# GpSimd's order in a slot: image normalising moved ahead of the finishes, and 24 gathers dealt out as 2, 4, 4, 4, 4, 4, 2

## The reference

```python
xn  = _gn(x)                                  # every channel of every image: (x - mean) / sqrt(var + 1e-5)
y   = conv7x7(xn, dilation 5, padding 15)     # 32 channels -> 1
imp = sigmoid(gelu(batchnorm(y)))             # importance of every pixel
xs  = xn * imp
idx = sort(top_k(imp, 192))                   # per image, in order of the pixel
tok = xs[idx] + pos[idx]                      # 192 tokens of 32 channels
t1  = ln(tok + attention(tok))                # 8 heads of 4 channels
t2  = ln(t1 + ffn(t1))
xn'      = xn
xn'[idx] = t2                                 # the tokens written back over their pixels
out = x + xn'
```

## Time and profile before

| | |
|---|---|
| median of 3 runs | 1338.59 us (1338.28 to 1342.16) |
| the profiled execution's own time | 1343.39 us |
| its span | 1341.5 us |
| mean granted TensorE clock | 0.869 of full |
| PE busy | 984.7 us (73%) |
| DVE busy | 904.1 us (67%) |
| POOL busy | 680.8 us (51%) |
| ACT busy | 662.5 us (49%) |
| moved by DMA | 246.88 MB, mean 184 GB/s |

### The profile page before, as it was taken

One profiled execution on the slowest core, in us unless ns is written; L12 is line 12 of the kernel. 1 busy time (PEld: TensorE's weight loads), 2 busy tenths in 40 slices (PEclk: granted clock), 3 DMA queues, 4 the chain that ended last, 5 costly groups with the idle time before them and its releaser, 6 DMA issues. The chain is left out here.

```text
span 1341.5 us, 21567 instructions
## 1 busy us (share of the span) xinstructions
PE 984.7 (73%) x6440; PEld 761.9 (57%) x6440; DVE 904.1 (67%) x2483; ACT 662.5 (49%) x1466; POOL 680.8 (51%) x949
## 2 busy tenths in 40 slices
PE   1397776688878978887888788877675676476647
PEld 1265555377656756775677667755553554355424
DVE  8145678678768867886788768975786675344523
ACT  1254342266436655765466546653653465256423
POOL 1043222822665386638663876286528547652553
PEclk9698897799879988999899979997987799599755
DMA  9488986575556888798879877855354454536558
GB/s 202 120 262 235 250 235 162 152 180 145 143 138 182 230 229 205 214 261 235 196 206 267 226 202 196 243 167 122 103 148 123 107 154 109 130 96 178 158 177 273
DMA packets 181223, 246.88 MB, mean 184 GB/s; under 512 B 70741, under 2 KB 77141, under 8 KB 181109
## 3 DMA queue, kind: packets, MB, share of 16 engines
q1 hardware_dynamic: 170613, 238.46, 65.9%
q10 hardware_dynamic: 2304, 4.65, 1.6%
q0 software_dynamic: 8192, 2.40, 1.3%
HBM read 123.61 MB, written 121.80 MB: 183 GB/s over the span
## 5 line engine op out<-in xcount | busy, mean ns | idle before, releaser
L534 PE MATMUL cv<-X,w_conv 128*128 128x330 f32 (+1 forms) x1024 | 315.3, 434 | 41.6 <-POOL X L974 36.7
L1018 POOL TENSOR_SCALAR res<-res,mom 128x440 f32<-128x440 f32 (+1 forms) x256 | 157.3, 616 | 329.7 <-DVE res L1314 321.2
L842 ACT ACTIVATE wgt<-ib,eps_col,mom 128x440 f32<-128x440 f32 (+1 forms) x256 | 176.5, 697 | 153.2 <-PE ib L581 144.9
L871 ACT ACTIVATE pr<-sc,least 128x192 f32<-128x192 f32 x384 | 140.6, 419 | 214.2 <-DVE least L1278 213.4
L534 PEld LDWEIGHTS cv<-X,w_conv 128*128 128x128 f32 x1024 | 196.1, 208 | 80.8 <-issue 43.4
L814 ACT COPY xt<-xb 110x512 f32<-110x512 f32 x225 | 132.7, 590 | 146.2 <-PE xb L518 110.3
L518 PE MATMUL xb<-cst,X 128*110 128x128 f32 x900 | 153.7, 298 | 68.8 <-ACT xt L814 48.6
L1314 DVE SCALAR_TENSOR_TENSOR res<-tr,mom,wgt 128x440 f32<-128x440 f32 (+1 forms) x192 | 122.4, 643 | 101.2 <-PE tr L568 94.6
L653 PE MATMUL sc<-k_b,qm 128*128 128x192 f32 x768 | 169.4, 346 | 20.2 <-ACT k_b L859 7.8
L666 PE MATMUL pp<-cst,pr 128*96 128x128 f32 x768 | 123.1, 284 | 66.9 <-ACT pr L871 49.5
L518 PEld LDWEIGHTS xb<-cst,X 128*110 128x110 f32 x900 | 105.9, 143 | 96.2 <-ACT xt L814 53.1
(11 more groups left out here) (173 smaller groups left out, 1476.7 us busy)
## 6 DMA issues: line engine op xcount, KB each, us to landing
table<-xt SPq DMA_DIRECT2D x240, 224.0 KB, 3.9
rt<-table SPq DMA_DIRECT2D x240, 224.0 KB, 4.5
out<-res SPq DMA_DIRECT2D x320, 137.5 KB, 2.9
X<-in_x SPq DMA_DIRECT2D x58, 412.5 KB, 6.1
X<-in_x SPq DMA_DIRECT2D x58, 343.8 KB, 5.2
conv_rows<-cvr SPq DMA_DIRECT2D x64, 188.0 KB
y<-conv_rows SPq DMA_DIRECT2D x64, 165.4 KB
out<-res SPq DMA_DIRECT2D x64, 68.8 KB, 2.9
```

Source lines behind the costliest of these rows:

```text
L534: last = mm(cv[:, 0:CUT[half]], w_conv[:, 4 * q + z], X[:, m % XI, at0:at0 + CUT[half]], start=z == 0, stop=z == 3)
L842: last = A(wgt[:, n % 2, at0:at0 + w], ib[:, at0:at0 + w], ACT.Identity, scale=mom[:, NB * g + b, 2:3], bias=eps_col[:, 1:2])
L871: last = A(pr[:, unit % 2, 2 * m + t, :], sc[:, k % 2, K * t:K * t + K], ACT.Exp, scale=-1.0, bias=least[:, k % 2, t:t + 1])
L1018: last = gp.tensor_scalar(v, v, 1.0, mom[:, NB * g + b, 0:1], ALU.mult, ALU.add)
```

## The change

GATHERS becomes (2, 4, 4, 4, 4, 4, 2): seven slots, phases 14 to 20. In GpSimd's loop the normalise stands first in the slot, ahead of finish, masked, norm_last, gather, scatter and split. No instruction is added or taken away, and no semaphore changes.

```diff
-        GATHER, GATHERS = 74, (3, 3, 3, 3, 3, 3, 3, 3)
+        GATHER, GATHERS = 74, (2, 4, 4, 4, 4, 4, 2)
...
                 if s == 27:
                     pool.wait_ge(dve_set, upto(dve_set, 0, 2))
                     gp.tensor_tensor(bn[:, 7:8], bn[:, 7:8], eps_col[0:H, 0:1], ALU.pow).then_inc(bn_rstd, 1)
+                for part in range(3):
+                    for g, b, n in images(s, NORMAL[part]):
+                        normalise(g, b, part)
                 for g, n in at(s, BACK, U):
                     finish(g, n)
...
                 for k in range(3):
                     for g, n in at(s, SPLIT[k]):
                         split(g, k)
-                for part in range(3):
-                    for g, b, n in images(s, NORMAL[part]):
-                        normalise(g, b, part)
```

## The result

| | before | after |
|---|---|---|
| median of 10 runs, same chip | 1341.55 us | 1348.99 us |
| lowest to highest | 1338.28 to 1343.11 | 1338.65 to 1351.67 |
| ratio after/before, 95% interval | | 1.0048 [1.0026, 1.0070] |
| profiled execution, its span | 1343.39, 1341.5 | 1349.58, 1347.8 |
| mean granted TensorE clock | 0.869 | 0.875 |

The changed kernel is slower by 0.48%: about 6.4 us by the ratio, 7.4 by the two medians. The forecast was 1336.0, the range ended at 1343.6. Of the 13 us between forecast and measurement, 3 lie in the base: the forecast started from the median of three runs of the kernel before, 1338.59, and ten runs give 1341.55. The rest is the effect of the change, forecast at -2.6.

What follows compares the result with a forecast made beforehand. No engine is full; work passes between engines each slot, with TensorE and VectorE waiting on GpSimd around the gathers. Terms -1.9 - 1.2 - 0.7 + 0.3 + 0.9 = -2.6 us from 1338.6 gave 1336.0 us, range 1330.5 to 1343.6.

Steps and rivals of the forecast that it cites:

- The scatters: Phase 5: second image's first third ahead of the last two scatters holds SyncE 2.6 us, delaying the search's map; +0.9 us.
- The prediction's own sign of being wrong: TensorE's wait falling over 1 us per group, or waits for table stores, loads back or the map in several groups.
- SyncE's hold comes through in full: Wait for the scatters at phase 6: 2.6 us in each of groups 0 to 3, 10.4; 1345.5 us, 11%.
- Fourth image: Phase 20, groups 2 to 5: first third normalised 0.48 us earlier, shortening TensorE's wait; -1.9 us over four groups.
- Group 1's second third: One normalise less stands ahead of it on GpSimd, so TensorE's 1.53 us wait nearly goes; -1.2 us.
- The gains as a sum: All forecast effects with SyncE's hold absorbed, so without the +0.9 of the scatters; -3.5 us.
- Group 0's later thirds: Group 0's normalising during the gathers: same as group 1, next to no wait on the second third; counted at nothing.
- Last gather: Groups 6 and 7, where the embedding waits for tokens: one finish less ahead; -0.7 in group 7, +0.3 in group 6.
- The rule on VectorE and GpSimd: Two-input VectorE instructions and GpSimd's SBUF reads exclude each other, so moved normalises could hold VectorE; put at nothing.
- the rival that asked for it once in each of six groups: Normalise holds an awaited VectorE instruction, 1.26 us once in each of groups 0 to 5; 1343.6 us, 4%.
- Clock kept up: Rival: shorter waits, mainly group 1's, keep TensorE's clock up, 2.8 us; with SyncE's hold absorbed 1332.3 us, 18%.

Runs made afterwards that it cites:

- the third experiment: The changed kernel with the second image's three normalises put back at the end of their slots; 1334.83 us, 0.9942 of the kernel before.
- the fourth experiment: The kernel before with only the second image's normalises moved to the front of their slots; 1353.88 us, 1.0092 of the kernel before.
- the gathers alone: The kernel before with only the gathers dealt out as 2, 4, 4, 4, 4, 4, 2, normalises last; 1364.71 us, 1.0180 of the kernel before.
- the move alone: The kernel before with all normalises first in their slots, gathers left at eight slots of three; 1344.28 us, 1.0015 of the kernel before.

## Why the prediction was wrong

- **The step that failed is "The scatters"**: +0.9 us for SyncE's hold. Moving the second image's normalises is worth 14 us taken away and 12 added on the first chip. The mechanism, its place and its victim (the map, VectorE's search) were named; the size was wrong, three times over. The prediction's own sign of being wrong, waits for the map in several groups, is there: three. First, SyncE is held longer than 2.6. Power, copies and normalise took 3.10 us (550.84 to 553.94), the finish 1.08 instead of 0.63, so the last scatter moved by 3.6 against VectorE's work, in groups 2 and 3 as well; in group 1 its landing took 1.4 longer too: 5 us. Second, I held this against slack read from before's schedule (1.2 of SyncE's idle time, 0.3 at the map). But the other steps of the change bring VectorE forward, by 6.6 us until slot 156, and what it asks for must come forward with it; slack against a schedule that moves is not slack. So group 2, with 2.3 us of idle time, lost 2.13 us, not 0.3, and group 3 lost 1.40. Third, the clock: the standstill of 4.94 us was followed by 6.8 us of work at 0.50, and from slot 156 to 165 the changed kernel lost 9.1 us where the wait by itself is 4.9. How much of the rest is the clock was not tried apart.
- **The rival "SyncE's hold comes through in full"**, 1345.5 us at 11%, named the right mechanism, and at +6.9 us came near the result's 6.4. That is luck, since two errors cancel: a hold of 10.4 us where the experiments show 12 to 14, and gains of 3.5 us where they show 7.8. And from the base of 1338.6 its 1345.5 lies 3.5 us under the measured 1348.99.
- **Fourth image, -0.48 a group**: right to the tenth, 0.22 us wait included. **Group 1's second third, -1.2**: right in the wait, 1.53 and a weight load's 1.94 giving way to 0.52.
- **The gains as a sum, -3.5 us without the hold**: too small. Without the hold the kernel was at 0.9942, -7.8 us. By slot 115 the lead was already 4.4 us, where groups 0 and 1 were to give 1.2. Of that lead the third experiment, with the other three images moved, has 2.4 us, and the fourth, with the second image alone moved, has 4.2: moving the second image's thirds also gained something, which I had not counted. Group 0's later thirds, counted at nothing, may hold a part; these are single executions, and it was not tried apart.
- **Last gather, -0.7 and +0.3**: right to where GpSimd ends, wrong behind it. GpSimd's last gathers of groups 6 and 7 after:

```profile
1035.19 0.93 POOL L1000 DMA_INDIRECT tok_pos<-in_pos,idx  x1 [0.31 <-issue]
...
1152.47 0.93 POOL L1000 DMA_INDIRECT tok_pos<-in_pos,idx  x1 [0.31 <-issue]
```

  and VectorE's embedding, against the earlier trace rows:

```profile
1039.53 0.48 DVE L1252 TENSOR_TENSOR tok<-tok_x,pp 96x128 f32<-96x128 f32 x2 [7.41 <-DMA tok_pos<-in_pos,idx]
...
1156.78 0.48 DVE L1252 TENSOR_TENSOR tok<-tok_x,pp 96x128 f32<-96x128 f32 x2 [13.05 <-DMA tok_pos<-in_pos,idx]
```

  From the first gather to the end of the last, group 7 took 33.0 us instead of 34.1, group 6 took 34.1 instead of 33.6. But the embedding starts 3.4 us after that end in both groups, where before it started 1.4 after (1148.62 against 1147.21 in group 7). So it is +0.9 for -0.7, and +2.5 for +0.3. It goes with the gathers: after, the gathers alone and the third experiment, which have four in a slot, show 3.4 to 3.6 in both groups; before, the move alone and the fourth experiment, with three, show 1.4 to 1.5. I had counted the gathers' issues and not their landings.
- **The rule on VectorE and GpSimd.** All normalises of the changed kernel (ns least/median/most):

```profile
L974 POOL TENSOR_SCALAR X<-X,mom x96: 1247/1257/1716, 26.4 to 912.9; 128x1100 f32<-128x1100 f32 x96
```

  The most was 1522 before. The longest are those of the second image's first third beside the masks of a search in groups 1, 2 and 3: 1.70, 1.71 and 1.72 us, each followed by a finish of 1.08. VectorE was in two instructions there that read two inputs from SBUF, and the second took 1.51 us in all three against 0.67 at the same places before. In group 1:

```profile
552.36 0.62 DVE L1135 TENSOR_TENSOR gt<-imp,tb 110x440 bf16<-110x440 f32 x1
552.90 1.51 DVE L1136 TENSOR_TENSOR eq_cg<-imp,tb 110x440 bf16<-110x440 f32 x1
```

  The Trainium skill (SBUF — State Buffer, Who interferes with whom) has it that the two exclude each other and the later one is blocked. The trace agrees for L1136, which ends 0.5 us after the normalise, and for the finish behind it, which ends 0.6 us after L1136. It does not for L1135: it started 0.12 us after the normalise and took its usual 0.62 us, and the normalise, which was there first, became 0.45 us longer. I had put all this at nothing because before's rows were even; they were even since no normalise ran at that place. So this term failed too. It cost GpSimd 0.9 us ahead of the last scatter, which is a part of the hold, and VectorE itself 0.84 us, three times: 2.7 us in the fourth experiment's slots, against 7.6 in the rival that asked for it once in each of six groups.
- **Clock kept up**: did not come. TensorE's wait in group 1 went, but new stalls at the map brought the low level back elsewhere.

## What to carry to other kernels

When part of a change brings one engine forward, read the slack of every transfer it will ask for against the new schedule: idle time in a queue covers a delay only as long as the consumer stays where it was. Before an instruction is moved to the front of an in-order engine's slot, list by slot what it now stands ahead of, and look for the one occurrence in the round that has a queue behind it; leaving the second image's normalises where they were (three of twelve here) turned +0.5% into -0.6% on one kind of chip. And measure on more than one chip: with the normalises first, four gathers a slot instead of three cost about 0.3% on one chip, and with the second image's last they cost 2.2% on another.

## What the runs showed of the hardware that I had not expected

- The same program differs by chip: before took 1341 to 1343 us on one kind, 1379 to 1387 on four others. The traces of the latter have waits of up to 17 us, with no recorded instruction or transfer at their end, inside series of indirect gathers or scatters; none over 1 us lies elsewhere.
- In groups 6 and 7 on the first kind of chip the last gather's data came 3.4 to 3.6 us after its issue had ended where four gathers stood in a slot, 1.4 to 1.5 where three did. In the move alone, where VectorE waited in every group, it was 1.4 to 2.9 with three.
- The landing of the last scatter is not even: 2.6 us from its end to the load back in group 1 of the changed kernel, 1.1 to 1.4 in groups 2 and 3 of the same execution.
- A wait of 5 us on VectorE was followed by 7 us at half the granted clock, while waits of 2.13 and 1.40 us in the same kernel were not (the clock was 1.00 from 718 to 724 us and from 854 to 862).
